# An early first operand stack, 17-wide values, scatters in bursts of eight, and weight loads under the last attention units

## The reference

```python
x = x + attn_a(layernorm(x))     # causal, with a decay -(i-j) added to the scores
x = x + ffn(layernorm(x))
x = x + attn_b(layernorm(x))     # causal, scaled
x = x + ffn(layernorm(x))        # 2 shared experts (mean) + top 6 of 32 routed experts, hidden 176
```

## Time and profile before

| | us |
|---|---|
| median of 3 runs | 3129.2 (3112.96 to 3131.95) |
| the profiled execution | 3135.21 |
| its span, first to last instruction | 3133.4 |
| PE busy | 2614.6 (83%) |
| DVE busy | 2075.2 (66%) |
| ACT busy | 1643.9 (52%) |
| POOL busy | 1395.5 (45%) |

### The profile page before, as it was taken

One profiled execution on the slowest core, in us unless ns is written; L12 is line 12 of the kernel. 1 busy time (PEld: TensorE's weight loads), 2 busy tenths in 40 slices (PEclk: granted clock), 3 DMA queues, 4 the chain that ended last, 5 costly groups with the idle time before them and its releaser, 6 DMA issues.

```text
span 3133.4 us, 72452 instructions
## 1 busy us (share of the span) xinstructions
PE 2614.6 (83%) x17832; PEld 1946.6 (62%) x17832; DVE 2075.2 (66%) x4624; ACT 1643.9 (52%) x2861; POOL 1395.5 (45%) x1046
## 2 busy tenths in 40 slices
PE   7699999999973799999385999999998728999992
PEld 5455565555553788888363555655555618888882
DVE  8666676776561687777395666766765517777872
ACT  3245444444411788888331554434444208888882
POOL 3430002314245688888544200023142457888885
PEclk9899999999987999999787999999999869999996
DMA  6975645555665789889859644564557648898988
GB/s 222 230 162 128 144 100 108 143 123 164 198 227 192 137 151 157 153 153 155 175 172 221 137 84 89 100 134 128 121 161 223 231 164 149 153 155 154 155 155 204
DMA packets 317281, 494.55 MB, mean 158 GB/s; under 512 B 55706, under 2 KB 225052, under 8 KB 311772
## 3 DMA queue, kind: packets, MB, share of 16 engines
q1 hardware_dynamic: 224908, 361.85, 43.9%
q0 software_dynamic: 92160, 130.08, 25.1%
HBM read 264.26 MB, written 256.77 MB: 166 GB/s over the span
## 4 chain that ended last, share of the span: by engine, by line
PE 45%; DMA 18%; issue 17%; POOL 6%; DVE 6%; SPq 3%; DVEq 2%; POOLq 1%; ACT 1%; ACTq 1%
PE ps L1576 10%; DMA expert_rows<-x 9%; PE ps L1590 9%; PE ps L1607 8%; DMA expert_sum<-x,route_u 5%; PE ps L1859 5%; PE ps L1877 4%; POOL expert_rows L1464 3%; PE ps L1594 2%; PE ps L1580 2%; SPq L424 2%; POOL expert_sum L1491 1%; DMA split<-rows_scratch 1%; DVE split L1171 1%; POOL split L1414 1%
## 5 line engine op out<-in xcount | busy, mean ns | idle before, releaser
L1282 ACT ACTIVATE work<-ps 128x1024 f32<-128x1024 f32 (+3 forms) x768 | 594.9, 810 | 679.0 <-PE ps L1594 458.1
L1464 POOL DMA_INDIRECT expert_rows<-x x372 | 365.4, 982 | 1272.1 <-DVE x L979 805.6
L1491 POOL DMA_INDIRECT expert_sum<-x,route_u x512 | 825.7, 1613 | 195.7 <-issue 92.5
L817 DVE TENSOR_REDUCE small<-ps 128x1 f32<-128x512 f32 (+3 forms) x1216 | 727.3, 656 | 216.9 <-PE ps L1580 145.1
L1576 PE MATMUL ps<-split 128*128 128x512 f32 (+3 forms) x1536 | 510.6, 408 | 72.3 <-DVE work L845 32.2
L1590 PE MATMUL ps<-split 128*128 128x512 f32 (+3 forms) x1536 | 501.6, 406 | 28.1 <-DMA split<-split 27.0
L1859 PE MATMUL ps<-split 128*88 128x256 f32 x3072 | 417.0, 285 | 86.2 <-DVE split L1171 50.4
L1859 PEld LDWEIGHTS ps<-split 128*88 128x88 f32 x3072 | 362.9, 155 | 134.9 <-issue 132.9
L1576 PEld LDWEIGHTS ps<-split 128*128 128x128 f32 x1536 | 275.0, 199 | 269.7 <-DVE small L817 144.8
L1877 PE MATMUL ps<-split 97*128 97x256 f32 x3072 | 408.8, 282 | 2.4 <-DVE split L1186 2.2
L1877 PEld LDWEIGHTS ps<-split 97*128 97x128 f32 x3072 | 384.7, 189 | 3.0 <-issue 2.9
(11 more groups left out here) (179 smaller groups left out, 3152.2 us busy)
## 6 DMA issues: line engine op xcount, KB each, us to landing
x<-expert_rows SPq DMA_DIRECT2D x256, 320.0 KB
split<-qks_scratch SPq DMA_DIRECT2D x192, 256.0 KB
qks_scratch<-split SPq DMA_DIRECT2D x64, 512.0 KB, 4.5
expert_rows<-in_pads SPq DMA_DIRECT2D x65, 320.0 KB, 16.0
v_scratch<-work SPq DMA_DIRECT2D x64, 256.0 KB, 4.3
split<-v_scratch SPq DMA_DIRECT2D x32, 512.0 KB, 14.3
xT_scratch<-split SPq DMA_DIRECT2D x16, 1024.0 KB
split<-xT_scratch SPq DMA_DIRECT2D x16, 1024.0 KB
```

The source lines that it names most:

```text
L817: v.tensor_reduce(cols[:, heads[0]:heads[0] + len(heads), i], ps[:, task_bank(n), 0:w * len(heads)].rearrange("p (h k) -> p h k", k=w), AX ...
L1282: c.activation(pexp[:, (s % 2) * 2 + h, :, BLK - w:], ps[:, 2 * h:2 * h + 2, BLK - w:], ACT.Exp).then_inc(s_pe, 1)
L1464: pool.indirect_dma_start(rows, bass.IndirectOffsetOnAxis(ap=posu[b][:, t * 8 + k:t * 8 + k + 1], axis=0), row_tile(b, t // TPB, t % TPB), ...
L1491: pool.indirect_dma_start(acc[r], bass.IndirectOffsetOnAxis(ap=idx[:, j, k:k + 1], axis=0), ye[:, r3, k, :], None, compute_op=ALU.add).the ...
```

## The change

Constants: at most 8 scatters in flight instead of 3, values 17 columns wide.

```diff
-AHEAD = 3
+AHEAD = 8
+VCOLS = NQB * HG * (HD + 1)
+VSLOT = VCOLS + 32
+VW = HD + 1
-    vds = nc.dram_tensor("v_scratch", (NU, P, NQB, HG * 32), F32, kind="Internal").ap()
+    vds = nc.dram_tensor("v_scratch", (NU, P, 2, TPB * HG * VW), F32, kind="Internal").ap()
```

```diff
-                    for f in range(2):
-                        last = v.tensor_copy(vst[:, r, :, 8 * f:8 * f + 8, 0:HD],
+                    for u in range(HG):
+                        last = v.tensor_copy(vst[:, r, u, :, :, 0:HD],
...
+                        at = (kb * HG + h) * VW
+                        last = mm(ps[32 * h:32 * h + 32, 6, BLK - w:], vreg[:, r, at:at + 32],
```

```diff
-                dve.wait_ge(s_pj, (L * NBLK + 4) * 6)
-                v.memset(stack32[64:P, 0, 0], 0.0).then_inc(s_zq, 1)
...
-                with pool.Fori(0, B - 1) as b:
+                with pool.Fori(0, B - 2) as b:
...
+                for o in range(2):
+                    p.memset(stack32[64:P, 0, o], 0.0).then_inc(s_zero[0], 1)
...
+                def first_stack():
+                    act.wait_ge(s_rowc, 16)
+                    act.wait_ge(s_zero[0], L * 2 + 2)
+                    for r in range(2):
+                        act.wait_ge(s_pd[r], (L * B + 1) * 64 + 64)
...
+                qkv_block(B - 2, 0, True)
+                first_stack()
+                qkv_block(B - 2, 1, True)
...
-                load_rows(0)
...
-                load_stack(0, 0)
-                store_block(B - 1, 0)
                 load_rows(1)
                 load_stack(1, 1)
-                store_block(B - 1, 1)
                 phase_end(sp, L, 0)
```

```diff
+                            burst = AHEAD // 2 if b < B - 2 else AHEAD
+                            if n and n % burst == 0:
+                                for i in range(n - burst, n):
+                                    r, m = divmod(i, TPB * TOPK)
+                                    pool.wait_ge(s_disp[r][m % AHEAD], ((L * B + b) * PER + m // AHEAD + 1) * 16)
```

```diff
                     v.tensor_tensor(xq, xq, summ[:, q], ALU.add).then_inc(s_ca[q], 1)
+                    if q == 0:
+                        first_quarter(L + 1)
```

```diff
+                    if u == NU - 2:
+                        sp.wait_ge(s_pv, (L * NU + NU - 3) * NS + NS + 2)
...
+                        sp.dma_start(raw.rearrange("p r n -> p (r n)"), wsd).then_inc(s_raw, 16)
+                        load_w2(16, 24)
+                        load_w2(27, 32)
...
-                    if u == NU - 1:
+                    if u == NU - 3:
                         sp.wait_ge(s_mr, TASKS + route_task(B - 2, 3) + 1 + 3)
```

More of the change, by code:

```diff
@@ L674, in _ @@
             dve.sem_inc(s_thl, 2)
-            chain = [0]
+            chain, layer = [0], [0]
             def link(ins):
@@ new lines, in normalise_block, with input_var @@
+            def normalise_block(N, blk, r):
+                dve.wait_ge(s_tp, N * NBLK + blk + 1)
+                for j in range(TPB):
+                    t = blk * TPB + j
+                    last = v.tensor_scalar(xn[:, r, j, :], x[:, ds(t * D, D)], sv[:, 8, ds(t, 1)],
+                                           sv[:, 9, ds(t, 1)], ALU.mult, ALU.add)
+                last.then_inc(s_xn, 1)
+            def input_var(N, q):
+                dve.wait_ge(s_x[q], 16)
+                dve.wait_ge(s_ca[q], N + 1)
+                apart(dve)
+                link(statistics(8 * q, 8))
+                linked()
+                row_var(stat[:, 8 * q:8 * q + 8, :], sv[:, :, 8 * q:8 * q + 8])
@@ L1209, in _ @@
                     v.tensor_tensor(xq, xq, summ[:, q], ALU.add).then_inc(s_ca[q], 1)
[L1210 removed]
+                    if q == 0:
+                        first_quarter(L + 1)
+            assert chain[0] == before + CHAIN, chain[0]
         @block.scalar
```

180 lines of the change are left out of this document (81 added, 99 removed).

## The result

The changed kernel takes 3108.2 us (median of 6 runs, 3097.4 to 3117.1) against 3130.6 for the kernel before beside it: a ratio of 0.9931, 95% interval 0.9908 to 0.9954. That is 22 us, where 70 were forecast. The profiled execution took 3109.9 (span 3108.0), against 3135.2 before.

The account below looks back on a forecast made before the run. It took PE in attention as the largest, unchanged part, then scatters, then value stores and constant rows at the projections' end. Terms -30 - 30 - 8 - 3 + 1 = -70 us against the 3129.2 median gave 3059, range 3028 to 3094.

Parts of the forecast that it names:

- Scatters of batches 2 and 3: Shared experts: bursts of eight end the scatter stage in 166 us instead of 181, -15 a layer, -30 in all.
- Rival 3: Shared experts: bursts of eight lose, stage 221 us, +40 a layer in place of -15, kernel 3169; chance 0.04.
- rival 2: Shared experts: bursts gain nothing, 96 scatters take their 181 us again, kernel 3089; chance 0.09.
- Early stack and 17-wide values: Projections' end: earlier first stack and narrower values bring first scores forward, -15 a layer, -30 in all.
- the -22: Projections' end, layer 0: without side effects first scores come at 140 in place of 162.09.
- The three debits: Projections: 4 us for stack loads delaying stores, 1 for ACT's issuing, 2 for POOL's zeroings; 7 off the gain.
- Rival 1: Projections' end: full DMA engines move the wait into blocks 6 and 7, gain -5 a layer, 3079; chance 0.15.
- the seam: Between the layers: quarter 0's work runs before quarter 1's sums land, PE's projections start earlier, -8 once.
- the end: Program's end: unused quarter work sits between DVE's two last adds, +1 (0 to +3).
- the moved weights: Attention: 5.1 MB of weight loads moved into a unit with DMA engines 16% busy, 0.
- Rival 4: Attention: weights loaded under unit 14 delay unit 15's maxima by 10 us a layer, kernel 3079; chance 0.05.

Follow-up runs that it names:

- e4: Changed kernel with the weight loads back at their old places; 0.9858 of the kernel before.
- e1: Changed kernel with batches 0 and 1 scattered three at a time again, batches 2 and 3 still in bursts of eight; 0.9864 of the kernel before.
- e13: Changed kernel with batches 0 and 1, beside attention, scattered at most eight in flight without a pause; 3273 us, 1.0473 of the kernel before.
- e2: Changed kernel with batches 2 and 3, in the shared experts, scattered at most eight in flight without a pause; 1.0296 of the kernel before.
- e5: Changed kernel with all scatters as before: batches 0 and 1 in threes, 2 and 3 at most three in flight; 3090 us, 0.9891 of the kernel before.
- e8: Changed kernel with the first stack's loads issued one block later on ACT; 0.9936 of the kernel before.

## Why the prediction was wrong

**The step that failed** is that attention stays as it is: "The largest is PE in attention (L1576, L1590, L1607), which the change leaves as it is", with the one term "In unit 10 of layer 0 DVE waits 4.05 for batch 0's scatters; bursts of four finish earlier: -3." It priced a burst by POOL's own queue alone. Measured were +14.2 and +3.6, 21 of the 45 us by which the two profiled executions miss the forecast. While POOL issues scatters back to back, what PE has finished reaches ACT and DVE late, in most cases until about 1 us after the burst. A burst of three is issued in 3.5 us (2 x 1.27 + 0.96), one of four in 4.8. In the routing units PE then idles, and its granted clock drops to 0.50 for some us more. Sixteen layers with bursts of four have U = 298 on the mean, fourteen with threes 290, the two before 290 and 291. Attention as a whole differs by 11 a layer, 22 us for the kernel; the ratios say 26, but between chips, and e4 on e1's chip shows nothing of it. That fours bring these waits and threes hardly any is shown on both chips that ran both, and that a longer run of scatters holds longer by e13 and e2; why PE's word waits is not. Ends of products are modelled in the trace, so whether the signal or the last product itself is late stays open. U with fours was 292 to 296 on one chip and 296 to 306 on the others. The waits go with it, 5.2 us a layer there and 10.4 on the others; why they are fewer there stays open.

**Scatters of batches 2 and 3, -15 a layer.** S fell by 5.1 and 8.8 in the changed kernel, by 9.3 on the mean of the 14 layers above (199.0 to 189.7): the direction is right, the term mis-sized. How much of it the bursts gave is not shown: e5, which takes them back, has 193.6 in layer 0, and in layer 1 the scatters without a pause hide what it would have. The scatters' own length was close, 173.6 in layer 0 and 167.3 in layer 1 in place of the 166 worked out, and POOL waited 53.8 for landings where the working implies 49 (11 x 2.33 + 23). Positions of batch 3 come at 925.1 in layer 0, where 914.60 was taken as the floor, and a burst waited 4.9 for them. Of these 10.5, 6.7 are the later start of the stage; the other 3.8 may be the bursts delaying their own supply, which was left out. Rival 3 did not occur; the truth lies between the forecast and rival 2.

**Early stack and 17-wide values, -15 a layer.** Measured -11, with the parts the wrong way round: the early stack, from which the -22 was worked out, is some 2 of it; the narrower values, counted as room for the stack, are in the other 9 together with SP's new order. Of the -22 worked out for layer 0, 13 did not come: 8.7 ahead of the maxima (120.68 in place of 112), the rest mostly in their load. The three debits were set at 4, 1 and 2. The trace shows 13.0 of DVE waiting for stores (2.77, 7.98 and 2.25), about 1 (36 products of a block took 9.50 beside ACT's issues, 8.43 in the next), and 6.9; they overlap, since they sum to more than the 8.7. Rival 1 had the mechanism of the first, stores pushed back at a full DMA share; its -5 for the whole was too little. That a zeroing holds DVE is a row now (6.87 beside 6.97, and 0.17 without). The Trainium skill, page "SBUF — State Buffer", section "Who interferes with whom", had said so; the trace agrees, and by that rule the sum would have been 8 later. That "first scores follow the load of the maxima by 2.9" failed as well: with the second stack in flight it is 4.8 to 8.2 by SP. That another queue does not help there (5.9 and 9.4 against 5.3) agrees with the Trainium skill, page "DMA: Bandwidth & Descriptors", section "Issuing engines are not separate DMA queues".

**Right:** the seam (-9.2 for -8), the end (+0.2 for +1), the moved weights (0 within what can be told). Rival 4 did not occur. Two sums of the rivals were wrong: by the working's own form (eleven bursts and seven issues) rival 3's stage is 212 and not 221, which gives 3152; and the 0.89 below 3098 holds 0.02 of rival 2's 0.09, which is not most of it.

A version beats the kernel before by more: the change with batches 0 and 1 left in threes, 0.986 of before on two chips, some 43 us faster.

## What to carry to other kernels

Price a run of GpSimd indirect DMAs by what the other engines do meanwhile, not by its own queue: beside dense TensorE work runs of three with a drain between them cost least here, and groups of four with shorter pauses did well in the shared experts. Before a transfer is moved earlier into a stretch in which the DMA engines are full, ask what it delays there; here the early place itself was worth some 2 of 11 us. In a trace, waits without a releaser that all end at the same distance from another engine's instruction are a lead.

## What the runs showed of the hardware

- Scatters issued without a pause nearly stop the core: PE busy 1.1 to 6.5 of some 20 us, one hand-off up to 34 us, at a DMA share of 0.36 to 0.38.
- Products that read 68 partitions instead of 128, with the same columns and PE as busy, had a granted clock of 0.71 over attention in place of 0.96, and 0.50 over the maxima; the zero rows that seem useless were worth some 430 us (3545.4 against 3112.4 for e8 on the same chip).
- Loads of a stack, into 16 or 20 partitions each, moved 118 GB/s at a DMA share of 1.03, stores from 128 partitions 366 at 1.01 (windows view of layer 1):

```profile
1664.00:1676.00 12.00, 9.35 (x39) 6.03 (x38) 10.31 (x19) 0.69 (x1) 11.01 (x6) 0.72 1.01 366
...
1684.00:1692.00 8.00, 5.78 (x19) 2.66 (x19) 7.42 (x16) 0.00 (x0) 0.00 (x0) 1.00 1.03 118
```
